# Cross attention and routed experts on one core: sums on four column tiles, work moved from VectorE to ScalarE and GpSimd, another order of VectorE's unit

## The reference, cut to what matters

```python
def reference(x, ctx_2048, Wg, bg, W1, W2):            # x, ctx: (4, 512, 512)
    # cross attention: 8 heads over the 512 rows of a batch, d = 64
    q, k, v = layernorm(x), ctx, ctx
    qn, kn = l2norm(q, per head), l2norm(k, per head)
    sm = softmax(5.0 * einsum('bhdq,bhdk->bhqk', qn, kn), axis=-1)
    x = x + einsum('bhqk,bhdk->bhdq', sm, vh)
    # routed experts: 2048 tokens, top 2 of 4, 512 tokens for each expert
    f = layernorm(x); logits = f @ Wg + bg
    for i in range(4):                                 # the 512 best tokens of expert i
        y = gelu(f[sel] @ W1[i]) @ W2[i] * p           # 512 -> 2048 -> 512
        out[sel] += y
    return x + out
```

## Time and profile before

| what | value |
|---|---|
| median of 3 runs | 617.82 us (615.79 to 618.09) |
| the profiled execution | 617.56 us, its span 615.8 us |
| PE, DVE, ACT, POOL busy | 580.6, 353.3, 281.2, 187.4 us |
| mean granted clock of PE | 0.973 |
| attention units 0 to 15 | 15 to 197 us |
| routing, gather | 197 to 247 us |
| experts | 247 to 616 us |

### The profile page before, as it was taken

One profiled execution on the slowest core, in us unless ns is written; L12 is line 12 of the kernel. 1 busy time (PEld: TensorE's weight loads), 2 busy tenths in 40 slices (PEclk: granted clock), 3 DMA queues, 4 the chain that ended last, 5 costly groups with the idle time before them and its releaser, 6 DMA issues.

```text
span 615.8 us, 8885 instructions
## 1 busy us (share of the span) xinstructions
PE 580.6 (94%) x2924; PEld 410.6 (67%) x2924; DVE 353.3 (57%) x698; ACT 281.2 (46%) x421; POOL 187.4 (30%) x142
## 2 busy tenths in 40 slices
PE   8999999999998735999999999999999999999994
PEld 4445555555554413788888888888888888888883
DVE  6889998998988683543444633444534255423212
ACT  3877777767776231533333334325324324333220
POOL 8465566466552226000300420400510401500002
PEclk9999999999999857999999999999999999999998
DMA  4523323323213125223323352333452522541001
GB/s 152 206 70 124 117 97 118 128 87 120 87 54 104 68 69 193 81 86 121 119 86 136 137 195 78 122 113 106 158 182 68 163 110 84 176 152 68 1 0 68
DMA packets 46600, 67.80 MB, mean 110 GB/s; under 512 B 8560, under 2 KB 25072, under 8 KB 46576
## 3 DMA queue, kind: packets, MB, share of 16 engines
q1 hardware_dynamic: 42736, 54.91, 26.5%
q0 software_dynamic: 3840, 12.59, 6.0%
HBM read 54.77 MB, written 12.64 MB: 109 GB/s over the span
## 4 chain that ended last, share of the span: by engine, by line
PE 69%; DVE 5%; DMA 1%; issue 1%; ACT 1%; POOL 0%; POOLq 0%; DVEq 0%
PE two L1478 29%; PE four L1508 9%; PE four L1507 9%; PE four L1505 9%; PE two L1310 3%; PE four L1300 2%; PE two L1322 1%; DMA x_got<-x2n_dram,idx_all 1%; DVE junk L1071 1%; PE four L1345 1%; PE bank_t L1338 1%; PE bank_t L1466 1%; PE bank_m L1466 1%; PE bank_t L1330 0%; PE four L1411 0%
## 5 line engine op out<-in xcount | busy, mean ns | idle before, releaser
L784 ACT ACTIVATE h_f<-two 128x512 f32<-128x512 f32 x64 | 38.3, 598 | 228.0 <-PE two L1478 228.0
L1240 DVE TENSOR_TENSOR h_lo<-h_f,h_hi 128x512 fp32r<-128x512 f32 x64 | 44.1, 690 | 122.8 <-ACT h_hi L785 122.8
L1478 PE MATMUL two<-xt_hi,w_hi 128*128 (+1 forms) x256 | 101.7, 397 | 0.7 <-ACT xt_hi L773 0.7
L1508 PE MATMUL four<-w_hi,h_lo 128*128 128x512 f32 x256 | 100.3, 392 | 0.0
L1507 PE MATMUL four<-w_lo,h_hi 128*128 128x512 f32 x256 | 100.3, 392 | 0.0
L1505 PE MATMUL four<-w_hi,h_hi 128*128 128x512 f32 x256 | 100.3, 392 | 0.0
L1478 PE MATMUL two<-xt_hi,w_lo 128*128 (+1 forms) x256 | 100.0, 391 | 0.0
L1478 PE MATMUL two<-xt_lo,w_hi 128*128 (+1 forms) x256 | 99.9, 392 | 0.0
L678 ACT ACTIVATE prob<-four,rnorm 128x512 f32<-128x512 f32 x128 | 77.6, 690 | 28.0 <-POOL rnorm L490 19.1
L1208 DVE TENSOR_TENSOR w_lo<-raw,w_hi 128x2048 fp32r<-128x2048 f32 x31 | 71.0, 2290 | 23.4 <-ACT w_hi L711 23.4
L490 POOL TENSOR_TENSOR rnorm<-ss_max,power 128x8 f32<-128x8 f32 x32 | 64.5, 2017 | 48.8 <-DVE ss_max L833 43.8
(11 more groups left out here) (183 smaller groups left out, 761.5 us busy)
## 6 DMA issues: line engine op xcount, KB each, us to landing
raw<-in_L_ffn_W SPq DMA_DIRECT2D x64, 512.0 KB, 4.2
x_all<-in_x SPq DMA_DIRECT2D x16, 256.0 KB, 2.7
c_sb<-in_ctx SPq DMA_DIRECT2D x16, 256.0 KB, 2.7
out<-x_all SPq DMA_DIRECT2D x16, 256.0 KB, 2.1
x2n_dram<-x2n SPq DMA_DIRECT2D x16, 256.0 KB, 2.0
p_inv<-inv_dram SPq DMA_DIRECT2D x30, 128.0 KB, 2.8
few<-p_sum SPq DMA_DIRECT2D x30, 2.0 KB, 2.1
cst<-in_consts SPq DMA_DIRECT2D x1, 423.5 KB, 5.2
```

Of the source, the lines that this page charges most:

```text
L784: nc.scalar.activation(h_f[m % 2][:, :], z_ps[m % 2][:, :], ACT.Gelu)
L1240: nc.vector.tensor_tensor(h_lo[m % 2][:, :], h_f[m % 2][:, :], h_hi[m % 2][:, :].bitcast(F32), ALU.subtract).then_inc(h_split, 1)
L1478: return nc.tensor.matmul(z[:, :], w_part[c][:, w], x_k, start=start, stop=stop)
L1508: last = nc.tensor.matmul(acc_ps[:, t, :], h_lo[m % 2][:, h], w_hi[c][:, w], start=False, stop=(m == MT - 1))
```

## The change

The sums of a unit (except the last) are four products into four blocks of 32 output rows, one for each half sum, without accumulation. `few` gets twice the columns, from four copies in place of two, and VectorE adds the two halves before the reciprocal. The high part of the queries and the widening of their norms are made by ScalarE. VectorE's unit has another order: queries, `normalize`, statistics (its small part later), `query_remainders`, `normalize_x2` of unit n-3 (it was n-2 at the end of the unit before), key squares, half sums, `invert_few`, query squares, half sums, logits, residual and statistics of x2. GpSimd makes `k_lo` of unit n+1 at the start of unit n and not of n+2 at its end. The low parts of both first chunks are made by GpSimd, in eight pieces with other waits. `find` has idle products between its quarters, and 20 follow it where 14 did.

The diff, with the context shortened:

```diff
@@ -37,6 +37,7 @@
 FEW = 2 * D // P
+QUAD = P // 4
 DVE_HEADS, POOL_HEADS = (0, 1), ()
@@ -200,7 +201,8 @@
             half_sum = [[att(f"half_sum{h}{n}", [P, D]) for n in range(2)] for h in range(2)]
-            few = att("few", [P, FEW])
+            few = att("few", [P, 2 * FEW])
+            few_sum = att("few_sum", [P, FEW])
             few_inv = att("few_inv", [P, FEW])
@@ -284,6 +286,7 @@
         few_in = sem("few_in")
+        few_added = sem("few_added")
         few_done = sem("few_done")
@@ -361,13 +364,15 @@
             unit((1, 1), 3, 3)
-            with engine.Fori(2, last - 1) as h:
-                unit((h, 0), 4, 3)
-                unit((h, 1), 4, 3)
-            unit((last - 1, 0), 4, 3)
-            unit((last - 1, 1), 4, 2)
-            unit((last, 0), 4, 1)
-            unit((last, 1), 4, 0)
+            unit((2, 0), 4, 3)
+            unit((2, 1), 5, 3)
+            with engine.Fori(3, last - 1) as h:
+                unit((h, 0), 5, 3)
+                unit((h, 1), 5, 3)
+            unit((last - 1, 0), 5, 3)
+            unit((last - 1, 1), 5, 2)
+            unit((last, 0), 5, 1)
+            unit((last, 1), 5, 0)
@@ -421,7 +426,9 @@
                     half = slice(h * P // 2, (h + 1) * P // 2)
-                    sp.dma_start(few[half, :], p_sum[DH * h:DH * h + 1, :]).then_inc(few_in, 16)
+                    for m in range(2):
+                        row = QUAD * (2 * m + h)
+                        sp.dma_start(few[half, m * FEW:(m + 1) * FEW], p_sum[row:row + 1, :]).then_inc(few_in, 16)
                 sp.wait_ge(few_done, n + 1)
@@ -516,14 +523,6 @@
-            def half_sums(u, n, h, reused):
-                pool.wait_ge(exp_done, TT * number(u) + 2 * n + 2)
-                if reused:
-                    pool.wait_ge(sums_ready, number(u))
-                nc.gpsimd.tensor_tensor(half_sum[h][n][:, :], prob[h][2 * n][:, :], prob[h][2 * n + 1][:, :],
-                                        ALU.add).then_inc(halves_done[h], 1)
@@ -564,29 +563,20 @@
             def unit(u, behind, ahead):
                 n = number(u)
-                for h in POOL_HEADS:
-                    if ahead:
-                        pool.wait_ge(rq_ready, n + 2)
-                    half_sums(u, 0, h, behind > 0)
+                if ahead and behind:
+                    pool.wait_ge(xn_done, n + 3 if ahead > 1 else UNITS)
+                    key_remainders(after(u))
                 if ahead:
...
                     key_norms(after(u))
-                for h in POOL_HEADS:
-                    if ahead > 1:
-                        pool.wait_ge(xsq_done, n + 3)
-                    half_sums(u, 1, h, behind > 0)
                 if ahead > 1:
...
                     finish(before(before(u)))
-                if ahead > 1:
-                    if behind > 1:
-                        pool.wait_ge(x2n_done, n - 1)
-                    key_remainders(after(after(u)))
@@ -594,9 +584,14 @@
             finish((UNITS // 2 - 1, 1))
-            for q in range(4):
-                pool.wait_ge(thr_done, q + 2)
+            pool.wait_ge(x2n_done, UNITS)
+            for q in range(2):
                 first_low(0, q)
+            pool.wait_ge(key_done, 2)
+            first_low(0, 2)
+            for q in range(3, 8):
+                pool.wait_ge(thr_done, q - 1)
+                first_low(q // 4, q % 4)
             pool.wait_ge(logit_done, UNITS)
@@ -666,6 +661,18 @@
+            def round_queries(u):
+                act.wait_ge(q_done, number(u) + 1)
+                nc.scalar.activation(q_hi[u[1]][:, :], q_f[:, :], ACT.Copy).then_inc(qhi_done, 1)
+            def widen_queries(u):
+                act.wait_ge(rq_done, number(u) + 1)
+                act.wait_ge(rq_ready, number(u))
+                nc.scalar.activation(wide_q[:, :, :, :], rnorm[u[1]][:, 1, :, :].unsqueeze(3)
+                                     .broadcast_to([P, TT, 2, DH]), ACT.Copy).then_inc(wq_done, 1)
@@ -694,7 +701,7 @@
                 if reused:
-                    act.wait_ge(few_in, 32 * n)
+                    act.wait_ge(few_in, 64 * n)
                 nc.scalar.activation(p_sum[:, :], o_ps[1][:, :], ACT.Copy).then_inc(sum_taken, 1)
@@ -717,6 +724,7 @@
             round_keys((0, 1), False)
+            round_queries((0, 0))
             act.wait_ge(rk_done, 1)
@@ -727,6 +735,8 @@
                     take_v(after(u), behind + 1)
+                if ahead:
+                    round_queries(after(u))
                 exponentials(u, 2, behind > 0)
@@ -738,6 +748,7 @@
                 if ahead > 1:
+                    widen_queries(after(after(u)))
                     round_keys(after(after(u)), True)
@@ -800,6 +811,10 @@
+            def gather_statistics(u):
+                n = number(u)
                 dve.wait_ge(bn_done, n + 1)
@@ -840,19 +855,19 @@
-            def queries(u, follow):
+            def queries(u):
...
                                                ).then_inc(q_done, 1)
-                nc.vector.scalar_tensor_tensor(q_hi[u[1]][:, :], x_norm[u[1]][:, :], ALPHA, bank_m[:, :],
-                                               ALU.mult, ALU.mult).then_inc(qhi_done, 1)
+            def query_remainders(u):
+                n = number(u)
                 dve.wait_ge(q_done, n + 1)
                 dve.wait_ge(qhi_done, n + 1)
-                if follow is not None:
-                    normalize(follow)
                 nc.vector.tensor_tensor(q_lo[u[1]][:, :], q_f[:, :], q_hi[u[1]][:, :].bitcast(F32), ALU.subtract
@@ -865,8 +880,11 @@
             def invert_few(u):
                 n = number(u)
-                dve.wait_ge(few_in, 32 * (n + 1))
-                nc.vector.reciprocal(few_inv[:, :], few[:, :]).then_inc(few_done, 1)
+                dve.wait_ge(few_in, 64 * (n + 1))
+                nc.vector.tensor_tensor(few_sum[:, :], few[:, 0:FEW], few[:, FEW:2 * FEW], ALU.add
+                                        ).then_inc(few_added, 1)
+                dve.wait_ge(few_added, n + 1)
+                nc.vector.reciprocal(few_inv[:, :], few_sum[:, :]).then_inc(few_done, 1)
@@ -919,14 +937,17 @@
             statistics((0, 0))
+            gather_statistics((0, 0))
             normalize((0, 0))
             statistics((0, 1))
+            gather_statistics((0, 1))
             sum_query_squares((0, 0))
...
             sum_query_squares((0, 1))
-            queries((0, 0), None)
+            queries((0, 0))
+            query_remainders((0, 0))
             widen_queries((0, 1))
@@ -937,6 +958,7 @@
             statistics((1, 0))
+            gather_statistics((1, 0))
@@ -994,15 +1016,24 @@
             def unit(u, behind, ahead):
+                if ahead:
+                    queries(after(u))
+                if ahead > 1:
+                    normalize(after(after(u)))
                 if ahead > 2:
                     statistics(after(after(after(u))))
+                if ahead:
+                    query_remainders(after(u))
+                if behind > 2:
+                    normalize_x2(before(before(before(u))), behind > 4)
                 if not ahead:
...
                 if ahead:
-                    queries(after(u), after(after(u)) if ahead > 1 else None)
                     sum_key_squares(after(u))
-                for h in DVE_HEADS:
+                if ahead > 2:
+                    gather_statistics(after(after(after(u))))
+                for h in range(2):
                     half_sums(u, 0, h, behind > 0)
@@ -1010,21 +1041,16 @@
                     normalize_x2(before(before(u)), True)
-                for h in DVE_HEADS:
+                for h in range(2):
                     half_sums(u, 1, h, behind > 0)
...
                     keys_of(0, EARLY)
-                if behind > 1 and ahead:
-                    residual(before(before(u)))
-                if behind > 1 and ahead:
-                    statistics_x2(before(before(u)))
-                if ahead > 1:
-                    widen_queries(after(after(u)))
                 if behind > 2:
...
                 if behind > 1 and ahead:
-                    normalize_x2(before(before(u)), behind > 3)
+                    residual(before(before(u)))
+                    statistics_x2(before(before(u)))
@@ -1220,8 +1246,6 @@
-            dve.wait_ge(wlo_done, 1)
-            split_lo(0, 1)
             for t in range(ST):
@@ -1319,8 +1343,15 @@
                     for h in range(2):
-                        last = nc.tensor.matmul(o_ps[1][DH * h:DH * (h + 1), :], cst[:, C_ONES:C_ONES + DH],
-                                                half_sum[h][n][:, :], start=(n == 0), stop=(n == 1))
+                        if ahead:
+                            row = QUAD * (2 * n + h)
+                            last = nc.tensor.matmul(o_ps[1][row:row + QUAD, :], cst[:, C_ONES:C_ONES + QUAD],
+                                                    half_sum[h][n][:, :], start=True, stop=True,
```

(14 more changed lines are left out.)

## The result

The changed kernel takes 649.99 us (648.04 to 650.47, 4 runs); the kernel before took 617.32 us in the same session (615.79 to 618.09, 4 runs). The ratio is 1.0517, with a 95% interval of 1.0486 to 1.0548. The profiled execution took 650.47 us, with a span of 648.5 us. The engines have hardly more work than before: TensorE is busy for 582.4 us where it was 580.6, VectorE for 10 us less and ScalarE for 12 us more, by the work moved between them.

What follows compares the result with a forecast made beforehand. TensorE and VectorE were both taken as full in the attention stage. From 617.56 us, plus 28.4 for the stall, less 3.4 for the low halves, plus 2 for the clock: 644.6, said as 645; range 634 to 658.

Steps and rivals of the forecast that it cites:

- The stall: Attention stage: the sums' copies queue on SP behind late x2n; unit 14.0 us, 28.4 us in all with the addition.
- rival 6: The faster case, attention stage: copies are there when VectorE reaches the inverse; unit 11.1 us, 603 us in all; chance 0.05.
- F: The moment in an attention unit when the copies of the sums have landed; the next landing was predicted at F+13.95.
- so in my schedule it costs nothing: GpSimd's moved k_lo ends at F+7.45, ahead of x2n at 7.65: no cost; 5 us if q_lo had to wait.
- rival 3: q_lo waits for k_lo in the attention units: 14.4 us a unit, 650 us in all; chance 0.07.
- The clock: TensorE's waits in attention units may lower its granted clock: 2 us taken, between 0 and 12 for 12 units.
- rival 2: The clock falls in nearly every attention unit: 14.6 to 15.2 us a unit, 651 to 662 us; chance 0.09.
- The sum: Whole kernel: 617.56 + 28.4 (stall) - 3.4 (low halves) + 2 (clock) = 644.6 us, said as 645.
- The low halves on GpSimd: Around the gather: chunk 3's load ends before it, tokens come 2 to 3 us sooner; saves 3.4 us, between 0 and 5.
- The four tiles: TensorE's sums on four column tiles take 1.01 us, a saving of 0.71 a unit, between 0 and 0.86.
- rival 5: Four tiles still run in pairs: sums take 1.87 us, x2n comes 0.3 later, 648 us in all; chance 0.03.

Runs made afterwards that it cites:

- The new queue order: Changed kernel with only SP's queue reordered: the four copies of the sums first, then the store of x2n and the loads of x and c; 603.9 us, ratio 0.9788.
- the kernel without the neighbour of q_lo: Changed kernel in which GpSimd's k_lo also waits for x2n, so that it doesn't run beside q_lo; 645.92 us, ratio 1.0485.
- the kernel with the clock held: Changed kernel with 12 idle products on TensorE in the wait ahead of each unit's sums; 647.89 us, ratio 1.0506.

## Why it came out as it did

**The stall: right, with its mechanism.** x2n, late in SP's fixed order, holds the loads and the copies, and these hold VectorE and TensorE. The new queue order takes 46 us off the changed kernel. The point from which the faster case was to decide, the copies there when VectorE reaches the inverse, is what that kernel reaches, and its 603.9 us are the 603 of rival 6, whose two parts come out near: the last inverse 8.9 us earlier for 10.8, the rest 4.3 shorter for 3.4. One unit by the steps of the prediction, in us from F: the changed kernel (additions at 103.54 and 118.60), and the kernel without the neighbour of q_lo (additions at 103.23 and 116.97):

| step | predicted | changed | k_lo after x2n |
|---|---|---|---|
| x2n ends after F | 8.2 | 9.16 | 8.24 |
| store of x2n to first copy | 1.89 | 1.76 | 1.86 |
| first copy to the addition | 3.81 | 4.11 | 3.61 |
| unit | 14.0 | 15.06 | 13.74 |

These are one of the longest and one of the shortest units. Over units 3 to 11 x2n ends at F + 8.96 on average in the changed kernel and at F + 8.26 in the other. From there to the next addition the changed kernel takes 14.71 - 8.96 = 5.75 us, which is what the prediction has (13.95 - 8.2). So SP's part of the sum was right, and all that was missed lies ahead of x2n's end.

**The step that failed: k_lo beside q_lo.** The prediction's "so in my schedule it costs nothing" was wrong. In the unit above q_lo starts beside k_lo and takes 1.39, not 0.69: q_hi was ready at 110.53 and q_lo started at 110.85, 0.44 us after k_lo did and 0.85 before its end at 111.70. In units 3 to 11 it takes 0.86 to 1.39 and is 4.9 us longer in all; it waited for q_hi in three of them, 0.3 to 0.45 us. All of the kernel (count, then the least, median and most in ns):

```profile
L871 DVE TENSOR_TENSOR q_lo<-q_f,q_hi x16: 692/1025/1394, 12.9 to 211.0; 128x512 fp32r<-128x512 f32 x16
```

My schedule had the two overlap as well (q_lo at F+7.05, k_lo until F+7.45); the cast in the earlier trace rows had shown what follows from it, and I let ScalarE's delay excuse it. This is rival 3, priced at 5 us: the kernel without the neighbour gains 0.54 a unit over units 3 to 11, again 4.9, and the medians differ by 4.1. The Trainium skill (GPSIMD Engine Reference, the specification table), which spoke for it, was right here.

**The clock: right in kind, a little small.** Over units 3 to 11 holding it gained 3.3 us, 1.9 of them through a shorter q_lo, where 2 stood for the whole stage; by the medians it is 2.1. A bound of 12 was needlessly wide, and rival 2, the clock lost in nearly every unit, did not come. In the unit above it is seen in the four transposes of c at 1.12 us, 0.66 at the full level in the kernel with k_lo after x2n, and as q_f waiting 0.54 for TensorE's spread.

**The sum.** Units 3 to 11 were to take 126.0 and took 132.4. The two causes by their own kernels make 4.9 + 3.3 = 8.2, but the 1.9 by which the held clock shortens q_lo is in both. Counted once, they make 6.3, and (132.4 - 6.3) / 9 = 14.0 is left for a unit, an estimate from these three traces (what the higher clock of the kernel without the neighbour gave it is not taken out). Unit 2's addition was 0.8 later than predicted (45.14 against 32.8 + 11.5 = 44.3), and units 12 to 15 took 48.0 where 49.0 was predicted. The last inverse was to come 28.4 + 2 = 30.4 later and came 34.7 later: 4.3 of the 5.9 us between 644.6 and the profiled 650.47.

**The low halves on GpSimd: right in kind, 1.5 us too much in this kernel.** The other part of the difference is the tail, 1.9 for 3.4. Alone it is worth 3.1 us by the ratio and 4.1 between the two traces, so the 3.4 holds. The tokens come 4.3 us sooner behind the start of the first gather, not 2 to 3: to the megabyte of chunk 3 comes the split of chunk 1, which the prediction put at nothing and which lengthened the gather's instruction by 1.08. No run takes away one of the two alone. In the changed kernel it saves the same between indices and first product, 10.6 us for 14.7 (269.35 to 279.92, 232.48 to 247.18) and loses 2.2 between the last inverse and the indices (43.6 us for 41.4). There TensorE works at a granted clock of 0.66 over 10 us (225.5 to 235.5; it was 0.98 from 191 to 201) after its wait of 2.96 us ahead of the last sums. Its timeline there, and at the indices and the first product:

```profile
227.67 3.68 PE L1353 MATMUL two<-half_sum,cst 128*64 128x512 f32 x8 [2.96 <-DVE half_sum L899]
231.10 2.97 PE L1334 MATMUL two<-prob,v_t 128*64 128x512 f32 x8
...
269.35 0.17 DVE L1210 TENSOR_SCALAR idx_all<-row 128x4 uint32<-128x4 f32 x1
...
279.92 0.50 PE L1511 MATMUL two<-xt_hi,w_hi 128*128 128x512 f32 x1 [0.69 <-issue]
```

The sums took 1.94 in the earlier trace rows and the weighted values 1.87 in the earlier trace rows. In the kernel with the clock held, which has no idle products in its last unit, the sums take 3.68 as well and the values 2.33, and its way from the last inverse to the end is 1.9 us shorter. That fits the clock as the cause, but only 0.6 of the 1.9 is seen in the values, and no run isolates it.

**The four tiles: right.** The sums are 1.0 us from start to next start (121.16 to 122.15, at the full clock; 106.10 to 107.18 is 1.08, where it begins to fall), with the 0.71 saved; so they don't run in pairs, as rival 5 had it. That they alone would bring 0.7 a unit was expected in the experiments and was wrong: the earlier trace rows had shown both engines nearly full, and only one of them was priced.

**What I had not seen.** That the move of k_lo gates the copies by itself; the prediction used this wait only for units 1 and 2, where it came out as said (unit 1 at 33.0 for 32.8).

## What to carry to other kernels

When an operation is moved later, follow it into every in-order queue that waits for it, and list what is queued behind it: here two such waits, x2n and k_lo, stood ahead of four 2 KB copies, and putting the copies first turned 5% slower into 2% faster. Where two engines are both full, price an edit on each of them; a saving on one is a wait for the other until both have it. Where an operation of VectorE is lengthened by a full-width one of GpSimd, as q_lo and x2n were here, don't rely on a schedule worked out that keeps them some tenths of a microsecond apart: order them with a wait, or price the overlap.

## What the runs showed of the hardware

VectorE beside GpSimd's k_lo (128x512, 1.3 us): q_lo, two inputs, 1.39 us for 0.69; x2n, one wide input, 1.50 for 0.55. They ended 0.54 and 0.29 us after k_lo did. The pairs of half sums beside the power on 8 columns kept 1.30. The Trainium skill (GPSIMD Engine Reference, the specification table) names VectorE instructions with two inputs in SBUF or in a two-port mode as those that contend with GpSimd; for q_lo the trace agrees, and whether x2n ran in such a mode no row shows.

Four column tiles in fp32 run together: four products of 512 columns in 1.0 us, where two accumulated pairs took 1.72. The first gather's instruction on GpSimd took 1.24 us without VectorE's 2048-column split beside it (in two kernels) and 2.32 with it. After TensorE's waits ahead of the sums, 1.6 to 3.7 us in units 3 to 11, the granted clock of a unit was 0.84 to 0.95 in six of the nine and 0.99 or more in three; after a wait of 2.31 us (the sums at 164.86) it was at the lower level, 0.50 of full speed, and after one of 3.35 us (those at 136.04) it stayed at the full one.
